# Keeping two chunks of up products in SBUF, making levels on GpSimd, and spreading the scale steps in a fused attention and quantised feed-forward kernel

## The reference, cut to what matters

```python
x = x + tanh(g_xattn) * xattn(layernorm(x), ctx)           # 16 heads, 16 x 256 tokens, D = 256
x = x + tanh(g_ffn)  * ffn(layernorm(x))
def act_qdq(x):                       # one scale for the whole tensor, 16 bits
    scale = max(max(abs(x)) / 32767, 1e-12)
    return clip(round(x / scale), -32768, 32767) * scale
def fixed_qdq_u16(x):                 # "levels": 65536 steps between 0 and 1
    return clip(round(x * 65536), 0, 65535) / 65536
def ffn(x):                           # D = 256, I = 768, weights in 4-bit blocks of 32
    x    = act_qdq(x)
    up   = act_qdq(x @ deq(w_up).T)
    gate = act_qdq(x @ deq(w_gate).T)
    gate = act_qdq(gate * fixed_qdq_u16(sigmoid(gate)))
    return act_qdq(gate * up) @ deq(w_down).T
```

## Time and profile before

| what | value |
|---|---|
| median of 3 runs | 616.76 us (614.8 to 617.37) |
| the profiled execution | 616.58 us, its span 614.7 us |
| PE busy | 564.1 us (92%) |
| DVE busy | 493.8 us (80%) |
| ACT busy | 439.0 us (71%) |
| POOL busy | 207.5 us (34%) |
| mean granted TensorE clock | 0.981 of full |

### The profile page before, as it was taken

The page is one execution under the profiler, slowest core; times in us unless marked ns, Lnnn a source line. Parts: engine busy times, 40 slices in busy tenths (PEclk is TensorE's granted clock), DMA queues, the critical chain, the costliest instruction groups (busy, mean ns, idle before and its releaser), DMA issues. The chain is left out here.

```text
span 614.7 us, 11698 instructions
## 1 busy us (share of the span) xinstructions
PE 564.1 (92%) x4315; PEld 339.9 (55%) x4315; DVE 493.8 (80%) x835; ACT 439.0 (71%) x632; POOL 207.5 (34%) x227
## 2 busy tenths in 40 slices
PE   2679999899999999999987899999999899949998
PEld 1345666566665666666445444444444344438887
DVE  5788889999999988998828599979988799954442
ACT  2237888678787777887766354549999998869860
POOL 4723347766666879755345000000000000010100
PEclk9889999999999999999999799999999999969999
DMA  6523344455544444433241000000000000023443
GB/s 192 133 87 116 102 127 130 120 144 134 144 132 138 125 132 127 119 81 106 66 116 53 2 1 1 0 1 1 1 1 0 1 0 1 1 69 104 138 138 103
DMA packets 42812, 48.98 MB, mean 80 GB/s; under 512 B 10436, under 2 KB 30532, under 8 KB 42756
## 3 DMA queue, kind: packets, MB, share of 16 engines
q1 hardware_dynamic: 40916, 43.38, 24.2%
q0 software_dynamic: 1408, 4.46, 2.6%
q10 hardware_dynamic: 432, 0.39, 0.3%
HBM read 24.32 MB, written 8.70 MB: 54 GB/s over the span
## 5 line engine op out<-in xcount | busy, mean ns | idle before, releaser
L872 DVE TENSOR_REDUCE negm<-s_ps 128x2 f32<-128x512 f32 x256 | 163.5, 682 | 25.2 <-PE s_ps L516 24.5
L695 ACT ACTIVATE pt<-st_ps 128x512 f32<-128x512 f32 x256 | 138.9, 596 | 54.8 <-PE st_ps L531 53.8
L1205 PE MATMUL pairs<-xq,wut 128*128 128x512 f16 x576 | 124.7, 379 | 2.7 <-ACT lnall L1357 1.6
L1205 PEld LDWEIGHTS pairs<-xq,wut 128*128 128x128 f16 x576 | 56.2, 98 | 71.1 <-issue 2.3
L516 PE MATMUL s_ps<-kst,qst 96*128 96x256 f16 x512 | 81.0, 274 | 11.0 <-DVE negm L872 7.6
L531 PE MATMUL st_ps<-qst,kst 97*128 97x512 f16 x256 | 76.5, 379 | 1.5 <-DMA qst<-mrow 0.9
L455 PE MATMUL pv_ps<-pt,vt 128*32 128x256 f32 x1024 | 68.5, 385 | 0.6 <-ACT pt L695 0.6
L1645 POOL PARTITION_ALL_REDUCE vmax<-vmax x5 | 1.8, 357 | 194.8 <-DVE vmax L1464 119.8
L516 PEld LDWEIGHTS s_ps<-kst,qst 96*128 96x128 f16 x512 | 46.0, 98 | 33.3 <-DVE negm L872 23.1
L1205 PE MATMUL pairs<-xq,wgt 128*128 128x512 f16 x276 | 60.5, 379 | 0.0
L1280 PE MATMUL pairs<-wdt,h 128*128 128x256 f16 x384 | 49.4, 281 | 8.4 <-ACT h L1393 8.4
(11 more groups left out here) (207 smaller groups left out, 1047.4 us busy)
## 6 DMA issues: line engine op xcount, KB each, us to landing
qst<-qk SPq DMA_DIRECT2D x96, 64.0 KB, 2.1
kst<-qk SPq DMA_DIRECT2D x45, 128.0 KB, 3.2
xt<-in_x SPq DMA_DIRECT2D x16, 256.0 KB, 4.3
ct<-in_ctx SPq DMA_DIRECT2D x16, 256.0 KB, 2.9
xr<-in_x SPq DMA_DIRECT2D x16, 256.0 KB, 3.9
out<-y SPq DMA_DIRECT2D x16, 256.0 KB, 3.8
lnall<-out POOLq DMA_DIRECT2D x8, 512.0 KB, 4.3
recb<-rec_dram SPq DMA_DIRECT2D x15, 256.0 KB
```

The costliest lines, as they stand in the source:

```text
L695: nc.scalar.activation(pt[:, (j // 2) % 2, j % 2, kt], st_ps[u % 3][:], ACT.Exp, scale=1.0 / (WS * WS * HD ** 0.5)).then_inc(exp_done, 1)
L872: nc.vector.tensor_reduce(negm[:, b % 2, tt, lo:lo + 5:4], s_ps[tt][:], AX.X, ALU.max, negate=True).then_inc(max_done, 1)
L1205: mm = nc.tensor.matmul(ps[:, p, k, :], w[:, a, dt, f * P:(f + 1) * P], xq[:, b, c, dt, :], start=n == 0, stop=n == len(terms) - 1)
```

## The change

Five things are done together.

1. **Two chunks kept.** In the first up pass, ACT copies the up products of chunks 2 and 5 from PSUM to SBUF (`keep_up`, six tiles; one chunk to a new buffer `ub`, one over `h3`). `up_max` of these chunks then reads SBUF and waits for the copy, and PE waits for the copy instead of the maximum before it reuses the place. In the second up pass PE makes six chunks instead of eight, and the chunks come in the order 2, 0, 1, 5, 3, 4, 6, 7.
2. **Levels on POOL.** Of each chunk's levels ACT makes one tile (two in the last chunk) and POOL the others, in place in `gb`, with two `tensor_scalar` per tile: times 65536 plus 2^23 (which rounds), then minus 2^23 and the minimum with 65535. The second waits for the first.
3. **Order on DVE.** `gated(c - 1, p)` now stands before `up_max(c, p)`; at the seam two of the last three `gated` stand before the wait for up's maximum; POOL's reductions stand between and behind its levels.
4. **Scales spread over steps.** In attention, the three instructions of `block_scales` stand in different steps, and so do the block maxima; clips are one step later.
5. **Unread products.** Six matmuls of 512 columns at the end of attention, and 24 between the second up pass and down (after the 22nd of 24 product tiles), whose results nobody reads.

```diff
-    SCALES = (2, 34, 66)
+    SCALES = ((-3, -2, 5, 5, 6, 6), (21, 22, 29, 30, 37, 38), (54, 61, 62, 69, 70, 71))
...
             nc.tensor.matmul(pv_ps[:, 1, 0:1], row1[:], ltop[:], start=True, stop=True).then_inc(ltop_spread, 1)
+            for _ in range(6):
+                nc.tensor.matmul(s_ps[0][:].rearrange("p a b -> p (a b)"), wo2[:, 0, 0, 0:P],
+                                 wo2[:, 0].rearrange("p a b -> p (a b)"), start=True, stop=True)
...
+    KEPT = (2, 5)
+    ORDER = (2, 0, 1, 5, 3, 4, 6, 7)
+    AGAIN = [c for c in ORDER if c not in KEPT]
...
-                    pe.wait_ge(u_max, PR * c + p + 1)
+                    if c - 1 in KEPT:
+                        pe.wait_ge(u_kept, kept_before(c - 1) + p + 1)
+                    else:
+                        pe.wait_ge(u_max, PR * c + p + 1)
                     products(wut, c, p).then_inc(u_done, 1)
...
+            pe.wait_ge(p3_done, PR * NC - 2)
+            spare_products(ps[:, 3, 1], 24)
...
+            def keep_up(c, p):
+                act.wait_ge(u_done, PR * c + p + 1)
+                nc.scalar.copy(kept_up[KEPT.index(c)][:, 2 * p:2 * p + 2], ps[:, p]).then_inc(u_kept, 1)
...
                 nc.scalar.activation(gb[:, c], ia[:, d], ACT.Sigmoid, scale=col(SG)).then_inc(sig_done, 1)
+                if c in KEPT:
+                    keep_up(c, 0)
                 act.wait_ge(sig_done, c + 1)
-                for p in range(1 if ahead(c, 1) else PR):
-                    part = slice(0, FT) if ahead(c, 1) else slice(2 * p, 2 * p + 2)
+                for p in range(level_tiles(c)):
+                    part = slice(2 * p, 2 * p + 2)
                     nc.scalar.activation(ib[:, d, part].bitcast(U16), gb[:, c, part], ACT.Copy, scale=LEVELS
                                          ).then_inc(sq_done, 1)
+                if c in KEPT:
+                    for p in range(1, PR):
+                        keep_up(c, p)
...
                 for p in range(PR):
+                    gated(c - 1, (c - 1) % 2, p)
                     up_max(c, p)
-                    if p == 0:
-                        dve.wait_ge(sq_done, c)
-                    gated(c - 1, (c - 1) % 2, p)
...
-            for n, i in enumerate((0, 4, 1, 2, 3)):
-                over_partitions(n, i)
+            over_partitions(0, 0)
+            def levels(c, p, n):
+                pool.wait_ge(sig_done, c + 1)
+                tile = gb[:, c, 2 * p:2 * p + 2]
+                nc.gpsimd.tensor_scalar(tile, tile, LEVELS, WHOLE, ALU.mult, ALU.add).then_inc(sums_done, 1)
+                pool.wait_ge(sums_done, n + 1)
+                nc.gpsimd.tensor_scalar(tile, tile, WHOLE, LEVELS - 1.0, ALU.subtract, ALU.min).then_inc(levels_done, 1)
+            n = 0
+            for c in range(NC):
+                if c == 1:
+                    over_partitions(1, 4)
+                for p in range(level_tiles(c), PR):
+                    levels(c, p, n)
+                    n += 1
+            for n, i in enumerate((1, 2, 3)):
+                over_partitions(n + 2, i)
```

More of the change, by code:

```diff
@@ L26 @@
 LEVELS = 65536.0
+WHOLE = 8388608.0
 def attention(nc, t, x, ctx, out):
@@ L952, in _ @@
                                                    op1=ALU.subtract).then_inc(wo_low, 1)
-                for i, at0 in enumerate(SCALES):
-                    if at0 - 1 - g in (16, 8, 0):
-                        part_scales(i, 2 - (at0 - 1 - g) // 8)
-                    if g == at0 - 1:
-                        if i:
-                            dve.wait_ge(blk_scaled, 2 * i)
-                        block_scales(i)
-                for i, n in pieces_behind(g, 4):
+                for i, steps in enumerate(SCALES):
+                    for p in range(PARTS):
+                        if g == steps[p]:
+                            part_scales(i, p)
+                    if g == steps[3]:
+                        scale_of_blocks(i)
+                    if g == steps[4]:
+                        inverse_of_blocks(i)
+                    if g == steps[5]:
+                        step_of_blocks(i)
+                for i, n in pieces_behind(g, 5):
                     if n // PARTS == 0:
@@ L1170, in ahead, with kept_before, level_tiles, sq_before @@
             return c + k < NC
+        def kept_before(c):
+            return PR * sum(k < c for k in KEPT)
+        def level_tiles(c):
+            return 1 if ahead(c, 1) else PR - 1
+        def sq_before(c):
+            return sum(level_tiles(k) for k in range(c))
         last_half = ps[:, 0, 0, 0:D]
@@ L1207, in products, with spare_products @@
                 return mm
+            def spare_products(bank, n):
+                for _ in range(n):
+                    nc.tensor.matmul(bank, wgt[:, 0, 0, 0:P], wgt[:, 0, 0, 0:CW], start=True, stop=True)
             first_turn()
@@ L1353, in _, with up_integers, gate_integers @@
             gate(NC - 1, 1)
-            def up_integers(c, p):
-                act.wait_ge(u2_done, PR * c + p + 1)
-                nc.scalar.activation(ia[:, c % 2, 2 * p:2 * p + 2, :], ps[:, p], ACT.Copy, scale=col(KU)
-                                     ).then_inc(qu_done, 1)
-            def gate_integers(c, p):
-                nc.scalar.activation(ib[:, c % 2, 2 * p:2 * p + 2], gb[:, c, 2 * p:2 * p + 2], ACT.Copy, scale=col(K2)
+            def up_integers(n, p):
+                c = ORDER[n]
+                if c in KEPT:
+                    source = kept_up[KEPT.index(c)][:, 2 * p:2 * p + 2]
+                else:
+                    act.wait_ge(u2_done, PR * AGAIN.index(c) + p + 1)
+                    source = ps[:, p]
+                nc.scalar.activation(ia[:, n % 2, 2 * p:2 * p + 2, :], source, ACT.Copy, scale=col(KU)).then_inc(qu_done, 1)
+            def gate_integers(n, p):
+                nc.scalar.activation(ib[:, n % 2, 2 * p:2 * p + 2], gb[:, ORDER[n], 2 * p:2 * p + 2], ACT.Copy, scale=col(K2)
                                      ).then_inc(q2_done, 1)
@@ L1379, in _ @@
                     up_integers(1, p)
-            for c in range(2, NC):
+            for n in range(2, NC):
                 for p in range(PR):
-                    act.wait_ge(p3_done, PR * (c - 2) + p + 1)
-                    gate_integers(c, p)
-                    up_integers(c, p)
+                    act.wait_ge(p3_done, PR * (n - 2) + p + 1)
+                    gate_integers(n, p)
+                    up_integers(n, p)
             act.wait_ge(chain, 2 + 3 + 3 + 3 + 3)
@@ L1548, in _ @@
                 for p in range(PR):
+                    gated(c - 1, (c - 1) % 2, p)
                     up_max(c, p)
[L1550 to L1552 removed]
             dve.wait_ge(u_max, PR * NC + PR)
             whole(1, PR * NC)
+            for p in range(PR - 1):
+                gated(NC - 1, (NC - 1) % 2, p)
             dve.wait_ge(all_max, 3)
             scale(vmax[:, 1, 1:2], UX, VX, SU, KU)
[L1557 to L1559 removed]
+            gated(NC - 1, (NC - 1) % 2, PR - 1)
             dve.wait_ge(p2_done, PR * NC + 2 * PR)
@@ L1583, in _ @@
             products(0, 0)
-            for n in range(1, PR * NC - 1):
-                products(n // PR, n % PR)
-                product_max((n - 1) // PR, (n - 1) % PR)
-            product_max(NC - 1, PR - 2)
-            products(NC - 1, PR - 1)
+            for m in range(1, PR * NC):
+                products(m // PR, m % PR)
+                product_max((m - 1) // PR, (m - 1) % PR)
             product_max(NC - 1, PR - 1)
```

59 lines of the change are left out of this document (41 added, 18 removed).

## The result

The changed kernel takes 657.1 us (median of 4, 654.2 to 657.5) against 615.8 us (614.3 to 617.4): ratio 1.066, 95% interval 1.062 to 1.070. The prediction, 620.5 us in a range up to 631, had the direction right and the size wrong by 37 us.

What follows compares the result with a forecast made beforehand. PE was taken to bound attention and down, ACT the first up pass, DVE the second. From 616.6 us: scales -2.5, first seam -1.0, library changes +7.2, port +2.2, second seam -2.0 gave 620.5 us; range 610 to 631.

Steps and rivals of the forecast that it cites:

- the price of POOL's instructions: First up pass: each of POOL's 30 level instructions takes 1.15 us, four of them 4.8 us under a 7.8 us chunk.
- POOL is slow: Rival, 5%: at 2.0 us or more per instruction POOL sets the first up pass; some 635 us, at 4.9 over 690.
- The port: First up pass: DVE's `gated` and POOL's instructions hold each other up; +2.2 us, bounds 0 and 7.
- The second seam: Between second up pass and down: 24 unread products let down start at full clock; -2.0 us.
- Scales: Attention: spreading `block_scales` over steps removes PE's waits behind DVE's maxima; -2.5 us, bounds 0 and -2.9.
- Library changes: POOL, first up pass and its seam: four more changes at 5.9 us each make levels and up's scale late; +7.2 us.
- POOL's levels at my price: First up pass and its seam: library changes and port together, +9.4 us.
- The cheap-change rival: Rival, 26%: going back to a POOL library used earlier costs little; 612.4 us, with a free port 610.2.
- The second pass: Second up pass: DVE sets 54.5 us before and after, so 15.5 us less work on PE is worth 0.
- The 0.7 us that the six products add to the barrier: First seam: six unread products ahead of the barrier end PE at 340.7 and make the barrier 0.7 us later.
- The stalls at kept chunks: First up pass: DVE loses 4.4 us at chunk 5, waiting for `keep_up`, and about as much at chunk 2.
- The first seam's clock: Attention to gate pass: clock held by six unread products -1.4 us, not held +0.7; taken -1.0.

Runs made afterwards that it cites:

- 1: Kernel before, with extra GpSimd `tensor_scalar` forms on a scratch tile in the gate pass and the second up pass; 614.9 us, one run.
- Experiment 2: Changed kernel with POOL's second instruction per tile as times 1, plus -2^23, leaving out the clip to 65535; 628.3 us, ratio 1.015.
- 8: Kernel before, with 24 POOL mult+add instructions on a scratch tile beside the first up pass, library changes in free time; 620.6 us, ratio 1.005.
- 11: Kernel before, with scales spread and unread products: six ending attention, five behind the barrier, 38 at the second seam; 611.6 us, ratio 0.989.
- 10: Kernel before, with scales spread and unread products at both seams (6 and 24); 614.6 us, ratio 0.994.
- 7: Kernel before, with one column's elementwise work on POOL ahead of up's reduction, forcing a library change at the seam; stretch 84.1 us.
- 6: Changed kernel with POOL's second instruction as times 1, plus -2^23, and no chunk kept; 626.0 us, ratio 1.015.
- 5: Changed kernel with all levels back on ACT and no chunk kept; 615.8 us, ratio 0.998.
- 4: Changed kernel with all levels back on ACT, two chunks still kept; 622.1 us, ratio 1.008.
- 12: On top of 11, two of three level tiles of chunks 1 to 5 in one POOL instruction each, reductions 1 and 2 first; 609.1 us, ratio 0.986.
- 9: Kernel before, with only the scales spread over steps; 614.5 us, ratio 0.996.

## Why the prediction was wrong

**The step that failed: the price of POOL's instructions**, "I take 0.2 plus the memset's 0.95, 1.15 us". For mult then add it was right (1.04 us by itself). For the second instruction of each tile it was 3.64. I had priced both by one number, and the nearest row stood among my bounds: the pointer row, 4.9 us for 1024 columns by its growth, which I had called far above. It was the only one of the three bounds that was a `tensor_scalar` at all, and its operations are subtract and mult, a pair that took 3.64 us in 1. The rival "POOL is slow" (5%) was what happened: its point of decision, 2.0 us, was passed by the mean of the two in the changed kernel, 2.75 us. It gave 635 at 2.0, and by its own four instructions in seven chunks it gives 656 at 2.75; 657.1 was measured. Experiment 2 shows the share of the price: 29 us.

**With the price that I had taken, the forecast was still low**: 628.3 for 620.5, or by the ratio 9.5 us over the kernel before where I had 3.9. In the stretch my sum came to 86.1 us and 2 took 90.8, so 4.7 us were missing there. Two terms had the wrong size.

- The port: `gated` took 8.3 us longer (2) and 8.1 us longer (8). My term of 2.2, between bounds of 0 and 7, was for what of this reaches the total, and that depends on who has slack: 3.2 us in 8, where ACT sets the pass, and more in 2, where DVE does (how much more, no run separates from the library changes). POOL's mult then add and DVE's two-input instruction do exclude each other. I had called `tensor_scalar` harmless by the row at 328 us, but that one is subtract and mult, a dear form, and DVE's instruction started 0.75 us into it. The Trainium skill, SBUF — State Buffer, section Who interferes with whom, has the loser wait out the whole instruction. For mult then add the rows of 2 agree (`gated` 2.04 us where 1.22 is usual, POOL 2.01 where 1.04 is). For subtract and min they do not: `gated` at 452.94 waited 0.9 us of 3.63, and here the measurement decides. Rows show both sides waiting, so the term is one for POOL too, and in the changed kernel, where POOL set the pass, that is where it told: 27.1 us for L1720 instead of 15.6.
- The second seam, -2.0: its "if the clock holds" failed. I had put the 24 products at 48.8 us plus 5.2 to 10.3 and looked only at whether they came too late. They took 5.3 us and ended 3 to 5 us too early. In the changed kernel and in five of six others with 24 the clock fell all the same, and the start of down was no faster than without them. With 38, and five more at the first seam, 11 is 2.9 us under 10 (0.0047 of 617).

**Right by mechanism and size.** Scales: -2.7 us of waits, -2.5 in time (interval -0.7 to -4.4), as predicted. Library changes: 6.0 us ahead of a reduction and 7.3 ahead of a `tensor_scalar` in the changed kernel, where I had 5.9 for each, paid again at each return; +6.7 us in 7. POOL's levels at my price cost 10.7 us in 6 against 5, where I had 9.4 with the stall at chunk 5 in it; how this divides between library and port, no run shows. The cheap-change rival (26%) is ruled out by 7. The second pass: 54.4 us of DVE, unchanged by two chunks less on PE. The 0.7 us that the six products add to the barrier: last attention product to first gate product 4.07 us, before 3.42.

**Right by mechanism, off in size.** The stalls at kept chunks, 4.4 us each: 6.9 and 3.5 in the changed kernel, 6.5 and 6.5 in 4. The first seam's clock, "held" or "not": in 4 of 7 profiles with six products it held (first 12 gate matmuls 2.75 us), in the 3 others not (4.44 in each). PE's gap behind the six is 1.5 us in all seven, so what decides is not shown. My -1.0 was a choice between the two, and the changed kernel's profile fell on the better side by luck.

**Not predicted.** DVE's new order costs: 5 and 10 differ in little else, and their stretches are 78.6 and 76.7, so 1.9 us. In 5 the last `up_max` ends 69.3 us after the first up product, in 10 it is 66.6; the two `gated` that stand ahead at the seam give 0.8 of these 2.7 us back. By the ratios it is +0.4% (0.998 against 0.994), with intervals that overlap. I had given the order no term.

## What to carry to other kernels

Price an elementwise instruction on GpSimd by its operations as well as its shape: until a row with the same two operations exists, the bound is the dearest row of the same kind, and it belongs inside the range. Look then at what it does per step of the loop, since a dear instruction that fits under the step costs nearly nothing and one that does not costs its whole excess. Give unread products an end time, not a count: those that reached up to the work they were for (gaps of 0.2 to 0.4 us, in 11 and 12) found the clock up each time, those that ended earlier only sometimes. And look for a stretch of the trace that repeats to a few hundredths when totals scatter by more than the effect.

## What the runs showed of the hardware

- GpSimd `tensor_scalar` with constants, 128x1024 fp32: 1.04 us for mult then add, 3.63 to 3.67 for five other pairs; at 128x512 0.62 for mult then add and 1.93 for subtract and min. With uint16 output mult then add (12) took 1.04 us at the least and 1.5 us in the mean. Why one pair is three times as fast, no run here shows.
- DVE's two-input instruction and GpSimd's one-input one wait for each other in both directions, up to 0.9 us for the first and 1.0 for the second; the dear forms hold DVE only near their start (three `gated` rows of the changed kernel, and DVE's products at 491.67 and 494.79 in 1). No experiment was made for this alone.
- A library change on GpSimd takes 5.9 to 6.2 us ahead of a reduction and 7.0 to 7.8 ahead of a `tensor_scalar`, at every return, and free time ahead of the next instruction's wait hides it (57 us of it in 7).
- Attention's end moves by some us from one execution to the next, in the same code: PE waits 2.1 to 2.6 us for DVE's `al` (L830) in five of the 14 profiles (before, 7, 8, 9 and the first of 4 and 5), 1.1 us in six, and not at all in three, the changed kernel's among them. In the kernel before, `al` (at 323.38) waits for ACT's `ah`, this for POOL's product at 321.43 (L1014), and this for a DMA. In 2, one of the six, DVE waits 0.3 us only, but `al` itself takes 1.68 us beside POOL's two-input instruction where 0.68 is usual. Why the DMA comes earlier or later, no run shows. So of the 4.6 us by which the changed kernel is ahead at its first up product, 2.4 may be this wait, and totals are compared by the ratios of many runs.
